# Compressed interaction layers of a recommender: one K tile packed fuller, a new order at the beginning, two copies moved to ScalarE

## The reference

```python
e = stack([tbl_f[ids[:, f]] for f in range(39)], axis=1)     # 2048 x 39 x 16
x = e
for W in (W0, W1):                                           # 128 outputs each
    inter = (x[:, :, None, :] * e[:, None, :, :]).reshape(B, last * 39, D)
    x = einsum('bid,hi->bhd', inter, W)
    outs.append(x.sum(axis=-1))
h = concatenate([outs[0], outs[1], dense_ctx], axis=1)       # 272 wide
h = relu(h @ W_top1 + b_top1); h = relu(h @ W_top2 + b_top2)
y = h @ W_top3
```

## Time and profile before

| | |
|---|---|
| median of 3 runs | 788.52 us (786.94 to 789.17) |
| the profiled execution | 789.04 us, its span 787.2 us |
| TensorE busy | 696.7 us (88%), 6210 matmuls |
| VectorE busy | 676.3 us (86%) |
| ScalarE busy | 420.1 us (53%) |
| GpSimd busy | 532.5 us (68%), all of it before 657 us |
| mean granted TensorE clock | 0.985 |
| transfers | 115.67 MB, mean 147 GB/s |

### The profile page before, as it was taken

The page is one execution under the profiler, slowest core; times in us unless marked ns, Lnnn a source line. Parts: engine busy times, 40 slices in busy tenths (PEclk is TensorE's granted clock), DMA queues, the critical chain, the costliest instruction groups (busy, mean ns, idle before and its releaser), DMA issues.

```text
span 787.2 us, 17029 instructions
## 1 busy us (share of the span) xinstructions
PE 696.7 (88%) x6210; PEld 594.9 (76%) x6210; DVE 676.3 (86%) x865; ACT 420.1 (53%) x769; POOL 532.5 (68%) x406
## 2 busy tenths in 40 slices
PE   0222477899999999999999999999999999999997
PEld 0221355687888888888888888888888888888887
DVE  5661699999999999999999999999999999988810
ACT  0001255656665666656565666565666656576641
POOL 6777788888878787878888888888887873000000
PEclk9997699999999999999999999999999999999999
DMA  4269869697876868686969676787878695754000
GB/s 106 66 133 271 152 161 182 164 163 170 171 160 151 144 172 144 169 157 163 182 160 169 152 169 134 182 139 184 135 182 142 162 167 154 160 151 132 14 7 1
DMA packets 171030, 115.67 MB, mean 147 GB/s; under 512 B 135043, under 2 KB 146906, under 8 KB 170563
## 3 DMA queue, kind: packets, MB, share of 16 engines
q1 hardware_dynamic: 156310, 110.49, 61.0%
q0 software_dynamic: 12800, 3.30, 6.2%
q10 hardware_dynamic: 1837, 0.78, 0.4%
HBM read 104.08 MB, written 15.53 MB: 152 GB/s over the span
## 4 chain that ended last, share of the span: by engine, by line
PE 76%; DVE 10%; DMA 4%; POOL 3%; issue 3%; SPq 3%; ACT 0%; DVEq 0%; ACTq 0%
PE z_ps L423 18%; PE x_ps L383 12%; PE x_ps L387 11%; PE x_ps L384 11%; PE g_ps L413 8%; DVE product_lo L671 5%; DVE products L663 4%; PE x1T_ps L444 4%; PE aux_ps L372 4%; POOL e_rows L359 3%; PE x1T_ps L402 3%; PE x1T_ps L436 2%; DMA id_spread<-id_scratch 2%; PE x1T_ps L434 2%; SPq L263 1%
## 5 line engine op out<-in xcount | busy, mean ns | idle before, releaser
L359 POOL DMA_INDIRECT e_rows<-in_tbl_dram,ids_sb x400 | 532.1, 1330 | 123.5 <-issue 119.5
L513 ACT CAST product_hi<-products 117x1024 fp32r<-117x1024 f32 (+1 forms) x256 | 242.7, 948 | 129.9 <-DVE products L663 126.9
L671 DVE TENSOR_TENSOR product_lo<-products,product_hi 117x1024 fp32r<-117x1024 f32 (+1 forms) x256 | 278.0, 1086 | 24.3 <-ACT product_hi L513 24.0
L663 DVE TENSOR_TENSOR products<-bases 117x1024 f32<-117x1024 f32 (+1 forms) x256 | 277.8, 1085 | 2.3 <-DMA bases<-eT_scratch 1.8
L383 PE MATMUL x_ps<-product_hi,w_hi 117*128 117x512 f32 x448 | 198.7, 444 | 10.5 <-ACT product_hi L513 5.9
L384 PE MATMUL x_ps<-product_hi,w_lo 117*128 117x512 f32 x448 | 178.3, 398 | 0.0
L423 PE MATMUL z_ps<-G,w1T 128*128 128x128 f32 x1248 | 178.1, 280 | 0.0
L423 PEld LDWEIGHTS z_ps<-G,w1T 128*128 128x128 f32 x1248 | 165.0, 191 | 17.3 <-issue 0.5
L387 PE MATMUL x_ps<-product_lo,w_hi 117*128 117x512 f32 x448 | 148.4, 401 | 29.5 <-DVE product_lo L671 29.4
L387 PEld LDWEIGHTS x_ps<-product_lo,w_hi 117*128 117x128 f32 x448 | 84.3, 190 | 54.6 <-DVE product_lo L671 34.7
L383 PEld LDWEIGHTS x_ps<-product_hi,w_hi 117*128 117x128 f32 x448 | 85.7, 191 | 24.9 <-issue 9.2
(11 more groups left out here) (54 smaller groups left out, 358.7 us busy)
## 6 DMA issues: line engine op xcount, KB each, us to landing
bases<-eT_scratch SPq DMA_DIRECT2D x155, 468.0 KB
e_diag<-e_scratch SPq DMA_DIRECT2D x512, 10.0 KB
id_spread<-id_scratch SPq DMA_DIRECT2D x16, 437.5 KB
e_rows<-in_tbl_dram,ids_sb POOLq DMA_INDIRECT x400
e_scratch<-e_d SPq DMA_DIRECT2D x16, 320.0 KB
eT_scratch<-e_rows SPq DMA_DIRECT2D x16, 312.0 KB
eT_scratch<-eT_scratch SPq DMA_DIRECT2D x16, 312.0 KB, 3.2
w1T<-in_L_rec_W_dram SPq DMA_DIRECT2D x1, 2496.0 KB, 16.4
```

The costliest lines, as they stand in the source:

```text
L359: nc.gpsimd.indirect_dma_start(out=e_rows[t % E_SLOTS][:, f * D:(f + 1) * D], out_offset=None, in_=tables[f], in_offset=bass.IndirectOffse ...
L513: nc.scalar.copy(product_hi[:, first:first + count, :], products[:, first:first + count, :]).then_inc(hi_ready, 1)
L663: nc.vector.tensor_tensor(products[:, first:first + count, :], bases[u % 2][:, b:b + count, cols], bases[u % 2][:, a:a + 1, cols].to_broad ...
L671: nc.vector.tensor_tensor(product_lo[:, first:first + count, :], products[:, first:first + count, :], product_hi[:, first:first + count, : ...
```

## The change

- The third block of the mixed K tile 3, until now unused in `product_hi`'s and `product_lo`'s matmuls, gets work. An eighth weight tile (`WT = NT + 1`) is prepared. A transfer issued by ScalarE in each chunk (`fill_mix`) copies block 0 of `product_hi`'s tile 3 into block 2 of `product_lo`'s tile 3. Two matmuls replace the three of this K tile: one on `product_hi`, with the low weights of block 0 or 1 packed where the block was free, and one on the filled `product_lo`. The second stands in group 3, after the wait for the transfer.
- `round_products(g+1, 1)` and `lower_parts(g+1, 1)` wait, further than before, for that second matmul of chunk g.
- The preparation masks the weights by block number: seven small VectorE instructions early, two on 117x256 later; the weights' transfers are 39 in place of 34.
- The beginning is in a new order: half of the small tables load from ScalarE's queue; `spread_ids(2)` goes before the first stores; the bases of chunk 1 load from ScalarE's queue; `w1T` and the tower's weights load after the block diagonals of chunks 0 and 3; the third rounding of the tables is joined with the subtraction before it.
- `copy_e` goes to ScalarE: `copy_e(t+1)` at the end of its chunk c = 0. The rounding of `dense_now` goes to ScalarE too, in chunk c = 1.

```diff
+MIX = 3
+WT = NT + 1
...
+    starts = [(BASES[a], BASES[b]) for a, b in PAIRS] + [(STARTS[0], (0, 13, 0))]
...
-            for n, f in enumerate(LOOKED):
+            for n, f in enumerate(LOOKED[:NS // 2]):
...
             spread_ids(0)
             spread_ids(1)
+            sp.wait_ge(zeroed, 1)
+            for n in range(3):
+                sp.dma_start(wt1_dense_f[n * GAP:n * GAP + D, :], w_top1[2 * H:2 * H + D, :]).then_inc(wt1_dense_loaded, 16)
+            spread_ids(2)
             store_eT(0)
             store_e(0)
             double_eT(0)
             sp.wait_ge(eT_doubled, 16)
-            for c in range(2):
-                load_base_part(0, c * (HB // 2), HB // 2, first_ready[c])
-
-            sp.dma_start(w1T[:, :, :], w1).then_inc(w1_loaded, 16)
...
-            spread_ids(2)
+            load_base_part(sp, 0, 0, HB // 2, first_ready[0])
...
                 spread(g)
+                if g == 0:
+                    sp.dma_start(w1T[:, :, :], w1).then_inc(w1_loaded, 16)
+                if g == 3:
...
                 for k in range(first, first + count):
                     nc.tensor.matmul(x1_ps[:, :], w0_hi[:, k, :], product_hi[:, k, :], start=(k == 0), stop=False)
-                    nc.tensor.matmul(x1_ps[:, :], w0_lo[:, k, :], product_hi[:, k, :], start=False, stop=False)
+                    if k != MIX:
+                        nc.tensor.matmul(x1_ps[:, :], w0_lo[:, k, :], product_hi[:, k, :], start=False, stop=False)
+                if n == NG - 1:
+                    pe.wait_ge(mix_filled, 16 * (g + 1))
+                    nc.tensor.matmul(x1_ps[:, :], w0_hi[:, NT, :], product_lo[:, MIX, :], start=False, stop=False).then_inc(mix_contracted, 1)
                 pe.wait_ge(lo_ready, g * NG + n + 1)
                 for k in range(first, first + count):
+                    if k == MIX:
+                        continue
                     last = nc.tensor.matmul(x1_ps[:, :], w0_hi[:, k, :], product_lo[:, k, :], start=False, stop=(k == NT - 1))
...
                 after(act, contracted, (g - 1) * NG + n + 1)
+                if first <= MIX < first + count:
+                    after(act, mix_contracted, g)
...
+            def fill_mix(g):
+
+                act.wait_ge(hi_ready, g * NG + 2)
+                act.wait_ge(lo_ready, g * NG + 2)
+                act.dma_start(product_lo[2:R:BLOCKS, MIX, :].bitcast(f32),
+                              product_hi[0:R:BLOCKS, MIX, :].bitcast(f32)).then_inc(mix_filled, 16)
...
+            copy_e(0)
+            act.wait_ge(eT_doubled, 16)
+            load_base_part(act, 0, HB // 2, HB // 2, first_ready[1])
...
+                if c == 1 and 0 <= t - 2 < TILES - 2:
+                    round_dense(t - 2)
                 if g < CHUNKS:
                     round_products(g, 2)
+                    fill_mix(g)
...
                 if g + 1 < CHUNKS:
                     round_products(g + 1, 1)
+                if c == 0 and t + 1 < TILES:
+                    copy_e(t + 1)
...
+                if first <= MIX < first + count:
+                    after(dve, mix_contracted, g)
...
+            nc.vector.tensor_scalar(w0_hi[:, mixed, :], w0_hi[:, mixed, :].bitcast(f32), is_other[0:R, :], None, ALU.mult).then_inc(w0_mixed, 1)
...
-            copy_e(0)
...
-                if c == 0 and t + 1 < TILES:
-                    copy_e(t + 1)
```

More of the change, by code:

```diff
@@ L85, in weight_runs @@
 def weight_runs():
[L87 to L90, removed]
+    starts = [(BASES[a], BASES[b]) for a, b in PAIRS] + [(STARTS[0], (0, 13, 0))]
+    for k, (a, b) in enumerate(starts):
+        for n in range(BLOCKS):
+            shift = (b[n] - a[n]) % F
+            start = a[n]
             if shift >= KT:
-                shift, start = F - shift, BASES[b][n]
+                shift, start = F - shift, b[n]
             yield n, k, start, shift, F - start
@@ L187, in cin_tower @@
         w0_split = sem("w0_split")
+        w0_mixed = sem("w0_mixed")
+        block_made = sem("block_made")
+        mix_filled = sem("mix_filled")
+        mix_contracted = sem("mix_contracted")
         w1_loaded = sem("w1_loaded")
@@ L235, in cin_tower, with load_base_part @@
         y_stored = sem("y_stored")
+        def load_base_part(queue, t, first, count, ready):
+            at = first % HB * D
+            for a, starts in enumerate(BASES):
+                step = starts[1] - starts[0]
+                part = eT_scratch[t, starts[0]:starts[0] + 1, first:first + count, :].rearrange("f b d -> f (b d)")
+                blocks = bass.AP(part.tensor, part.offset, [[TB * D, F], [step * TB * D, BLOCKS], [1, count * D]])
+                queue.dma_start(bases[first // HB][:, a, at:at + count * D], blocks).then_inc(ready, 16)
         block = ctx.enter_context(nc.Block())
@@ L254, in double_eT @@
                 sp.dma_start(eT_scratch[t, F:2 * F, :, :], eT_scratch[t, 0:F, :, :]).then_inc(eT_doubled, 16)
[L256 to L263, removed]
             def load_bases(u):
@@ L555, in copy_y, with copy_e, round_dense @@
                 nc.scalar.copy(y, mlp_ps[0:1, 2, :]).then_inc(y_ready, 1)
+            def copy_e(t):
+                act.wait_ge(gathered[t % E_SLOTS], (t // E_SLOTS + 1) * 16 * len(GATHERED))
+                act.wait_ge(looked_up, (t + 1) * sum(map(len, SETS)))
+                after(act, e_stored, 16 * t)
+                nc.scalar.copy(e_d[:, :, 0:F], e_rows[t % E_SLOTS][:, :].rearrange("b (f d) -> b d f", d=D)).then_inc(e_d_ready, 1)
+            def round_dense(t):
+                act.wait_ge(dense_loaded, (t + 1) * 16 * 3 * GAP // D)
+                after(act, h1_in_ps, M1 * t)
+                nc.scalar.copy(dense_parts[:, :], dense_now[:, :]).then_inc(dense_hi_ready, 1)
+            for n, f in list(enumerate(LOOKED))[NS // 2:]:
+                act.dma_start(tab_f[:, K_FIRST[n] * D:K_FIRST[n + 1] * D], tables[f].rearrange("(p k) d -> p (k d)", k=K_OF[n])).then_inc(tab_loaded, 16)
             act.wait_ge(zeroed, 1)
@@ L598, in _ @@
                     round_products(g + 1, 1)
+                if c == 0 and t + 1 < TILES:
+                    copy_e(t + 1)
+                if g == CHUNKS - 1:
+                    round_dense(TILES - 2)
+                if g == CHUNKS + CPT:
+                    round_dense(TILES - 1)
             copy_y(TILES - 1)
@@ L602, in _ @@
         def _(dve):
-            def copy_e(t):
-                dve.wait_ge(gathered[t % E_SLOTS], (t // E_SLOTS + 1) * 16 * len(GATHERED))
-                dve.wait_ge(looked_up, (t + 1) * sum(map(len, SETS)))
-                after(dve, e_stored, 16 * t)
-                nc.vector.tensor_copy(e_d[:, :, 0:F], e_rows[t % E_SLOTS][:, :].rearrange("b (f d) -> b d f", d=D)).then_inc(e_d_ready, 1)
             def make_one_hot(t, n):
@@ L646, in split_dense @@
             def split_dense(t):
-                dve.wait_ge(dense_loaded, (t + 1) * 16 * 3 * GAP // D)
-                after(dve, h1_in_ps, M1 * t)
-                nc.vector.tensor_copy(dense_parts[:, :], dense_now[:, :]).then_inc(dense_hi_ready, 1)
                 dve.wait_ge(dense_hi_ready, t + 1)
@@ L706, in _ @@
             dve.wait_ge(tab_loaded, 16 * NS)
-            for part in range(PARTS):
+            for part in range(PARTS - 1):
                 after(dve, tab_split, 2 * part)
                 nc.vector.tensor_copy(tab[:, part, :], tab_f).then_inc(tab_split, 1)
-                if part < PARTS - 1:
-                    dve.wait_ge(tab_split, 2 * part + 1)
-                    nc.vector.tensor_tensor(tab_f, tab_f, tab[:, part, :], ALU.subtract).then_inc(tab_split, 1)
+                dve.wait_ge(tab_split, 2 * part + 1)
+                rest = tab[:, PARTS - 1, :] if part == PARTS - 2 else tab_f
+                nc.vector.tensor_tensor(rest, tab_f, tab[:, part, :], ALU.subtract).then_inc(tab_split, 1)
             dve.wait_ge(lookup_ready, 4)
```

50 lines of the change are left out of this document (33 added, 17 removed).

## The result

The changed kernel took 804.53 us (802.01 to 811.35) where the kernel before took 788.85 in the same comparison: a ratio of 1.0213, 95% interval 1.0146 to 1.0280. The whole interval lies above 1, so the kernel is slower: by 2.1%, give or take 0.7. The time is outside the range of 751 to 780. The profiled execution took 804.02 us, its span is 802.2.

What follows compares the result with a forecast made beforehand. TensorE was taken to bound the steady tile. Its way: 21 + 2.4 + 11 x 0.47 + 7 x 0.23 = 30 us gained, span 757; GpSimd's later 763.8 sets the end, giving 765 us, range 751 to 780.

Steps and rivals of the forecast that it cites:

- What bounded the kernel before: Steady tile: TensorE, busy all 42.54 us, sets the pace, VectorE 1.4 us behind; GpSimd has only a lead.
- Matmuls: TensorE, each chunk: 21 matmuls become 20, gaining 0.23 us a chunk, 0.92 a tile.
- The fill: ScalarE's transfer into product_lo each chunk: small loads landed in 2.3 to 4.9 us, so covered by 1.8 to 4.6.
- rival D: The fill lands in 7 us, TensorE waits about 0.7 in each chunk, 45 us less 23 gained: 810; chance 0.11.
- The new semaphore and ScalarE's copy of e: At c = 0 the held rounding and a 0.7 us copy delay x1: 0.45 us lost a tile (0.35 to 0.8).
- VectorE's held remainder: VectorE's lower_parts(g+1, 1), held to about 475.7, has room to spare: charged 0, at most 0.5 us a tile.
- The beginning: Earlier spread_ids(2) removes VectorE's 22.48 us stall; 1.5 us (0 to 5) come back, a gain of 21.
- rival C: The beginning gives part back: store_eT(1) late behind bases and w1T, a stall of 2 to 8 us: 774; chance 0.17.
- GpSimd's way to the end: Gathers slowed beside VectorE's products, 42.3 us a tile, use up their lead and set the end: span 763.8.
- Rival B: TensorE alone sets the time, the gathers keep up: 758, or 753 with no wait for x1; chance 0.26.
- the signs: Profile after: no VectorE stall above 5 us, tiles of 42 to 42.5, copies 1.4 to 3 behind gathers, last gather near 664.
- the five outcomes: Forecast 0.42, Rival B 0.26, rival C 0.17, rival D 0.11, no change that counts (789) 0.04.

Runs made afterwards that it cites:

- packed_free: The changed kernel without the in-chunk transfer, the second packed matmul in group 1 so nothing is held (one product missing): 765.72 us, 0.9733.
- no_fill: The changed kernel without the in-chunk transfer and TensorE's wait for it, rounding still held (one product missing): 776.39 us, 0.9846.
- start_only: The kernel before with the new order of the beginning alone: 781.69 us, 0.9922.
- bases_small: The changed kernel with SP's base loads in the loop cut to a sixteenth, most products on old data: 770.88 us, 0.9775.

## Why the prediction was wrong

**What bounded the kernel before**: right. TensorE's tile of 42.54 is what the runs without the packing keep (42.52 in no_mix).

**Matmuls**, 0.23 each, 0.92 a tile: right. packed_free shows 0.88.

**The fill**, the step that failed. I took 2.3 to 4.9 us for its landing from small loads at the very beginning, while the steady DMA share of 0.76 stood in the earlier trace rows, and called it covered by 1.8 to 4.6 us. The room was about right: from the end of the rounding at 466.7 to 474.24 are 7.5 us, and TensorE leaves 6.8 to 8.1. The landing was not. With 0.6 to 0.8 for the issue I had 2.9 to 5.7 us; where L401 waited in a steady tile, it could start only 7.3 to 8.9 us after the issue began. The fills are late in every second chunk, as the bases come, and in steady tiles TensorE waits in every fourth. It is rival D, with its place right (TensorE waits for the filled `product_lo`), its landing of 7 us near, and its time of 810 as well, but that time is in part luck. D had 0.7 us of wait in each chunk, 45 in all. Measured are 30.6, half of them in the first four late fills and about 1 us a tile from then on, with some lower clock behind the waits; and the gain of 23 that D set against its 45 did not come. What I had not seen is the loop: the hold ties the issue of the next fill to L401, so the room never grows (no run has the fill without the hold, so what more room would give is not shown). The Trainium skill, "DMA: Bandwidth & Descriptors", section "Queues, rings and completion order", has each engine turn between queues packet by packet, which I read as in favour of the forecast. Here the fill's first packet on ScalarE's own queue ends 4.5 us after the issue behind SP's bases and 1.6 without them: an own queue does not pass the other's backlog by itself. A packet of that page is several descriptors of one queue, 9 to 17 as it says, and not one of the 2 KB pieces that the profile counts here, so it does not say that a small transfer gets through at once. How the turns were taken here stays open.

**The new semaphore and ScalarE's copy of e**: right in kind, and inside its bounds of 0.35 to 0.8. The wait for `x1` at c = 0 is there, 0.74 where I had 0.45. The copy takes 1.29 us, not 0.7 and outside my bound of 1.06, which came from a row with another access pattern.

**VectorE's held remainder**, charged 0, at most 0.5: right for this kernel. In no_fill, which has the hold and the copies on ScalarE, TensorE's idle time in a steady tile is all for `x1`. It would not hold with the copies on VectorE: there a tile is about 1 us longer than without the hold (42.62 against 41.66), with VectorE's remainder as the wait. That includes VectorE's copy, so how much is the hold's alone was not parted further.

**The beginning**, 21: wrong in size. It gives 6.5 by itself, 8.2 by the spans (779.0 against 787.2). The chain of `id_spread` was as forecast: in the kernel after it is issued at 32.91, and the first products start at 62.19, within 59 to 63. What I called rival C, the beginning giving part back, is what happened, through the gathers of tile 1 and not through the stores behind `w1T`.

**GpSimd's way to the end**, which was to set the end at 763.8: wrong for the steady state. In start_only and packed_free the last gather of a tile gets further ahead of its copy, from 8.8 to 32.0 us and from 7.4 to 28.9. The pace of 42.03 that I read from the earlier trace rows was no limit of GpSimd's: in start_only its tiles 5 to 15 are 40.9 apart (637.68 less 228.86, the ends of two last gathers, by 10). That gathers are slower beside VectorE's products did hold: in start_only, after 200 us, all 106 gathers of more than 1.4 us ran beside `products` and `product_lo`. Rival B was right that the gathers keep up: after tile 3 no copy waited for them in any of these runs. That the time of packed_free is the 765 that I forecast is chance, as it has no hold and no fill, and another limit.

**Of the signs** that I named: no stall of VectorE over 5 us in the loop over chunks (the longest is 4.9; one of 22.6 stands at the very end, where the kernel before has 15.6), the issue before 40, 64 matmuls fewer and waits for `x1` at c = 0 came, and the sign of rival D, TensorE waiting on the filled `product_lo`. The copies 1.4 to 3 us behind the last gather did not come, since they stand 8.7 to 46 behind from tile 1 on; nor did tiles of 42 to 42.5, or a last gather that ends near 664 (654.6). (The chances of the five outcomes add up to 0.85 for faster and 0.11 for slower; I wrote 0.86 and 0.10.)

What is left to gain: **no_mix**, the change less its packing, is faster than both kernels, 779.27 us, 0.9898 (0.9874 to 0.9922). By packed_free, which has no fill, the packing is worth at most 779.27 - 765.72 = 13.6 us on top of it, if the fill is early and nothing is held. A second buffer of the mixed tile should do away with the hold, and then the fill could be issued earlier and have more room; it was not tried.

## What to carry to other kernels

A transfer that is produced and used within one stage has to be priced by its landing in the busiest moment of that stage, read from the queue that is full just then, and never by the landings of the quiet beginning. If a wait is added behind such a transfer, follow it around: where the next issue hangs on the use of this one, the room for each transfer is fixed (here 7 to 8 us), and no lead can be built up that would absorb a late one. A few busy moments are then enough: one wait of about 1 us in a tile, on the engine that sets the pace, is more than the 0.92 that the change saves there. And a stall that is removed at the beginning uncovers whatever was waiting beside it, so the gain is the distance to the next-latest input, here the gathers.

## What the runs showed of the hardware

- ScalarE's copy of 128x624 floats in a strided order takes 1.29 us (1.27 to 1.30 in 16 of them), VectorE's 0.69 to 0.85, although ScalarE's 128x512 in order, from `x_ps`, takes 0.59 and its rounding of 117x1024 1.05.
- SP needs about the same time to issue a load of 117 rows whether it is 468, 234 or 29 KB: 0.93 and 0.83 us each in the rows above, and 0.81 in bases_small.
- A gather that GpSimd issues in the same rhythm of 1.25 us can land 9.7 us after it began, at a DMA share of 0.92 (start_only, 70.17 to 79.87). At the beginning the store that needs a last gather followed 2.4 us after it began, 39.63 less 37.26, at a share of 0.03 to 0.09.
- TensorE's granted clock fell for 3.4 us after four of its waits for the fill in steady tiles (after waits of 1.2 to 2.0 us; after others of up to 1.5 us it did not). Windows of the kernel after, and below them one of packed_free, which has no such wait:

```profile
316.00:320.00 4.00, 2.37 (x25) 1.92 (x23) 3.76 (x5) 0.92 (x2) 3.39 (x3) 1.00 0.75 191
320.50:324.00 3.50, 3.50 (x42) 2.99 (x43) 1.92 (x3) 1.53 (x2) 2.89 (x3) 0.69 0.34 101
```

```profile
320.00:324.00 4.00, 4.00 (x27) 3.38 (x27) 3.97 (x8) 2.71 (x6) 3.21 (x3) 1.00 0.86 240
```

Before 320 TensorE is busy for 2.37 of 4 us, and after that the mean is 0.69, that is, part of the stretch is at the 1.2 GHz level. Three of the four stretches lie in the ten tiles that were compared with no_fill. Each costs at most half of its 3.4 us, 5.1 together, of the 18.6 that these tiles lost.
